# Perceiver layer: context handed over channels first, values' weights loaded beside the queries, exponentials two pieces ahead

## The chip, the core and the metric

One core of a Trainium2 chip runs the whole program. The metric is the device time of one launch in microseconds, the median of the runs. TensorE (PE, with PEld for its weight loads), VectorE (DVE), ScalarE (ACT) and GpSimd (POOL) each work through a queue of their own in program order; SyncE (SP) issues most DMAs. They meet only through semaphores written out by hand.

## What is computed

A layer with a cross-attention, a self-attention and a mixture of experts, each added to `x`. The change touches the first, and the ends of the queries' stage in front of it.

```python
def cross_attention(text_hidden, vision_tokens, vision_mask, Wq, Wk, Wv, Wo):   # (2,256,512), (2,4096,256)
    q = (text_hidden @ Wq).reshape(B, T_text, 16, 128).transpose(0, 2, 1, 3)
    k = (vision_tokens @ Wk).reshape(B, T_vis, 8, 128).transpose(0, 2, 1, 3)    # each used by 2 query heads
    v = (vision_tokens @ Wv).reshape(B, T_vis, 8, 128).transpose(0, 2, 1, 3)
    scores = einsum('bhtd,bhsd->bhts', q, k) / sqrt(128)
    attn = softmax(where(mask, scores, -inf))
    return einsum('bhts,bhsd->bhtd', attn, v) ... @ Wo
x = x + cross_attention(layernorm(x), ctx_1024, mask, ...)
x = x + self_attention(layernorm(x), ...)
x = x + experts(layernorm(x), ...)
```

## The kernel before

The program has four blocks that follow one another: `queries`, `cross`, `selfattn`, `experts`. Every fp32 factor of a product is split into a high part (a copy rounded to fp32r, made by ACT) and a low part (the rest, made by DVE or POOL by a subtraction), and each product is three matmuls: low by high, high by low, high by high.

`queries` layer-norms `x`, makes the queries of all 16 heads, and stores them in DRAM. Beside this SP loads the context of batch 0, raw, into `prob`, 16 pieces of 256 KB (`context_piece`, L144).

`cross` works on one batch after the other. Its pieces:

- `first_part(b)` makes the values. The context arrives with the tokens on the partitions, so PE turns it by transposes against an identity (`context_turn`, L925): 8 blocks of 512 tokens, each with 2 x 4 transposes into two banks of the PSUM ring of 4 (`ring`). ACT copies a bank to `ctxh` (`context_high`, L626), DVE subtracts to `ctxl` and frees the bank (`context_low`, L786). The values' weights are loaded by SP at the start of the block in batch 0 (L404, `values_weight`), ACT makes their high part (`values_weight_high`, L633), DVE the low part (`values_weight_low`, L791). `values_make` (L937) makes 64 products of six matmuls over 512 columns, in two passes (`quad` 0 and 1) over the 32 chunks of 128 tokens; DVE copies each from the ring (`values_out`, L800) and SP stores them in pairs to `v_dram` (L417). DVE waits in `values_out` until the store of the pair two before has landed (`v_st`). The block's turn comes `CTX_LAG` = 2 loop steps after its load and its values `V_LAG` = 4 steps after it.
- `group(...)` makes keys (`keys_make`, L945) and scores (`score`, L956) of head pair u+1, while it turns the exponentials of pair u (`turn`, L965: four transposes per chunk k of 128 tokens, 32 chunks) and multiplies them with the values (`pv`, L975, two chunks later). In a group u = 8b + g - 1. Its chunk k on ACT is the copy `pt_high` (L589), on DVE the subtraction `pt_low` (L741). There are PT = 3 banks for the turned chunks: `turn(k)` waits for `pt_low(k-3)`, and `pv(k)` for `pt_low(k)`.
- The exponentials are in place in `prob` and `more`, [128 rows, 4096 tokens] for each of four tiles t. `exp_piece(u, n, t)` (L575) does one piece of one tile; the pieces are token blocks 0, 1, 2, 3-4, 5-6 and 7 (`PIECES`), and `turn(u, k)` waits at the first chunk of a piece until all four tiles of it are done (k = 0, 4, 8, 12, 20, 28). Piece 0 comes ahead of the group; the others stand in ACT's queue beside the chunks right in front of their use (`BESIDE`, `exp_ahead`), so piece 1 goes with chunks 0 to 3, and turn(4) needs its last quarter.
- Six of the seven groups of a batch that have `pv` run in a loop (g = 2 to 7) and start with two `keys_make` and four `project` (L914, the output product of the pair before). The group of g = 1 (`op` false) has no `project` in front of its first turn.
- Group 8b - 1 for b = 1 has its turns and products inside `first_part(1)`, beside the values of batch 1; there the context's loads go piece by piece into the parts of `prob` that were just turned (SP waits for `pt_full`). The very last group (u = 15) has turns, `pv` and no scores.

`more` is a tensor of `cross` alone; `prob` is shared with the blocks around it.

Of the kernel before, what the change touches and what calls it, by code (L numbers as in the profile page):

```python
# [13 lines left out]
P = 128  # L14
# [95 lines left out]
def queries(nc, x, wq, ctx_in, q_dram, X, ident, prob):  # L110
# [6 lines left out]
    with ExitStack() as ctx:  # L117
# [118 lines left out]
def cross(nc, ctx_in, mask, wk, wv, wo, q_dram, v_dram, attn_w, X, ident, prob):  # L236
# [19 lines left out]
    BESIDE = {1: (0,), 2: (1,), 3: (2,), 5: (3, 4), 7: (5, 6)}  # L256
# [6 lines left out]
    CTX_LAG, V_LAG = 2, 4  # L263

    def ctx_at(n, c):
        return c if n == 0 else (n * 2 + c if n < 2 else 4 + (n - 2) * (CC + NC) + 2 + c)

    def v_at(n, q):
        if n < SB - 2:
            return 4 + n * (CC + NC) + q + (CC if q >= 2 else 0)  # L270
        return 4 + (SB - 2) * (CC + NC) + (n - (SB - 2)) * NC + q

    FIRST = CC * SB + SCH * QUADS
# [27 lines left out]
    with ExitStack() as ctx:  # L301
# [6 lines left out]
        more = t_.sb("more", [P, RT, S])  # L308
# [22 lines left out]
        def wv_raw(quad):  # L331
            return more[:, :, (0, 3)[quad] * BANK:((0, 3)[quad] + 1) * BANK]
# [11 lines left out]
        def wv_part(ring, quad, c):  # L344
# [7 lines left out]
                 "pv_done", "o_hi", "o_lo", "mask_ok", "inv_chain", "any_chain", "scores_seen")  # L352
# [21 lines left out]
        def ctx_count(b, n, c):  # L374
            return b * ((CC + HKV) * SB) + n * CC + c + 1

        def k_count(b, u, n):
            return (b + 1) * (CC * SB) + u * SB + (n + 1)
# [14 lines left out]
        def _(sp):  # L393
# [30 lines left out]
            for b in range(B):  # L424
                u0 = b * HKV

                if b == 0:
                    values_weight(0)
                    values_weight(1)
# [8 lines left out]
                for n in range(SB + V_LAG):  # L438
                    if b and n < SB:
# [6 lines left out]
                        if n == 3:  # L446
                            sp.wait_ge(s["wv_ld"], (b * QUADS + 1) * 16)
                            values_weight(1)
                        if n >= 2:

                            sp.wait_ge(ctx_ld[n % 2], n // 2 * (RT * 16))
                        for r in range(RT):
                            sp.dma_start(*context_piece(prob, ctx_in, b, n, r)).then_inc(ctx_ld[n % 2], 16)
# [3 lines left out]
                    if n >= V_LAG:  # L457
                        for q in range(NC):
                            values_store(b, (n - V_LAG) * NC + q, 0, v_at(n - V_LAG, q))
# [4 lines left out]
                for n in range(SCH):  # L464
                    values_store(b, n, 1, CC * SB + SCH + n)
# [102 lines left out]
        def _(act):  # L568
# [8 lines left out]
            def exp_ahead(u, n, q):  # L577

                for at, blocks in BESIDE.items():
                    if n in blocks:  # L580
                        chunk = blocks.index(n) * NC + q
                        if (chunk + 1) % len(blocks) == 0:
                            exp_piece(u, at, chunk // len(blocks))
# [1470 lines left out]
```

## Time and profile before

| | us |
|---|---|
| median of 3 runs | 2091.35 (2087.42 to 2095.75) |
| profiled execution, device time | 2088.11 |
| its span | 2086.2 |
| PE busy | 1974.1 (95%) |
| DVE busy | 1137.2 (55%) |
| ACT busy | 988.0 (47%) |
| POOL busy | 314.4 (15%) |

In the trace the queries end at 63.5, `cross` runs from 66.7 to 1487, with batch 1 from 727 on, then come self-attention and the experts. PE is the engine that is busy nearly all the time, so what counts is how much work PE has and where it stands still. A row of the timeline gives start, duration, engine, line, what it writes and reads, how many like instructions are merged, and in brackets the idle time of that engine just before, with what ended it. The time between the starts of two rows is what an instruction costs its engine; the duration of one matmul is longer, since they are pipelined.

### The profile page before, as it was taken

The page shows a single profiled execution, that of the slowest core. Times are in us where ns is not written, and L with a number is a line of the kernel's source. Part 1 is how long each engine was busy: PE and PEld are TensorE (multiplying, and loading weights), DVE is VectorE, ACT ScalarE, POOL GpSimd, SP SyncE. Part 2 cuts the span into 40 slices and gives each one's busy share as a digit, 9 for nine tenths or more (in the row PEclk, how much of TensorE's full clock was granted, in tenths as well). Part 3 has the DMA queues.
Part 4 walks back from the last instruction along what each step waited for, and adds up shares of the span by engine and source line. Part 5 has one row for each costly group of instructions (what it writes and reads, how often), then busy time and mean ns, then how long its engine had stood idle before and what let it go on. Part 6 is the DMA issues. An engine that isn't in the chain of part 4 may idle for free. (4 is left out here: it accounts for less than half of the span.)

```text
span 2086.2 us, 32487 instructions
## 1 busy us (share of the span) xinstructions
PE 1974.1 (95%) x10420; PEld 1634.4 (78%) x10420; DVE 1137.2 (55%) x2532; ACT 988.0 (47%) x2092; POOL 314.4 (15%) x252
## 2 busy tenths in 40 slices
PE   7899999999999989999999999998698899999998
PEld 5687877877877778878777877877564588999997
DVE  3457676666666655666676666766757531000002
ACT  3202766665676572055665666676435342122111
POOL 0200111211211113011112211211314210000001
PEclk9899999999999999999999999999899999999999
DMA  7452111111111145501111111102200816466542
GB/s 217 164 188 85 35 45 38 35 48 38 48 31 39 41 134 181 180 24 44 36 43 38 34 48 38 49 25 62 86 0 0 294 57 251 177 243 259 203 177 63
DMA packets 127151, 198.09 MB, mean 95 GB/s; under 512 B 12461, under 2 KB 69989, under 8 KB 122976
## 3 DMA queue, kind: packets, MB, share of 16 engines
q1 hardware_dynamic: 123120, 188.59, 27.3%
q10 hardware_dynamic: 2672, 4.55, 0.7%
q0 software_dynamic: 1280, 3.93, 0.6%
q8 instruction: 46, 0.75, 0.2%
q14 instruction: 33, 0.27, 0.0%
HBM read 151.50 MB, written 45.81 MB: 95 GB/s over the span
## 5 line engine op out<-in xcount | busy, mean ns | idle before, releaser
L741 DVE TENSOR_TENSOR crs_ptl<-crs_tp,crs_pth 128x512 fp32r<-128x512 f32 x512 | 352.7, 689 | 228.2 <-ACT crs_pth L589 227.7
L589 ACT ACTIVATE crs_pth<-crs_tp 128x512 fp32r<-128x512 f32 x504 | 300.6, 597 | 283.7 <-PE crs_tp L965 280.5
L510 POOL TENSOR_TENSOR crs_vl<-crs_vraw,crs_vh 128x512 fp32r<-128x512 f32 x128 | 165.0, 1289 | 1110.5 <-ACT crs_vh L596 1110.5
L965 PE MATMUL crs_tp<-all_ident,crs_prob 128*128 128x128 f32 x1024 | 199.4, 277 | 39.5 <-ACT crs_more L575 39.5
L956 PE MATMUL crs_ring<-crs_kh,crs_ql 128*128 128x512 f32 x512 | 235.3, 460 | 0.0
L965 PEld LDWEIGHTS crs_tp<-all_ident,crs_prob 128*128 128x128 f32 x1024 | 140.9, 141 | 116.3 <-ACT crs_more L575 55.6
L975 PE MATMUL crs_ov<-crs_ptl,crs_vh 128*128 128x512 f32 x512 | 210.5, 411 | 2.0 <-DVE crs_ptl L741 1.5
L975 PE MATMUL crs_ov<-crs_pth,crs_vh 128*128 128x512 f32 x512 | 203.5, 397 | 0.0
L956 PE MATMUL crs_ring<-crs_kh,crs_qh 128*128 128x512 f32 x512 | 202.9, 396 | 0.0
L956 PE MATMUL crs_ring<-crs_kl,crs_qh 128*128 128x512 f32 x512 | 202.1, 395 | 0.0
L975 PE MATMUL crs_ov<-crs_pth,crs_vl 128*128 128x512 f32 x512 | 201.7, 394 | 0.0
L965 PE MATMUL crs_tp<-all_ident,crs_more 128*128 128x128 f32 x1024 | 197.8, 275 | 0.0
L575 ACT ACTIVATE crs_prob<-crs_prob,crs_nmax 128x512 f32<-128x512 f32 (+1 forms) x192 | 165.1, 860 | 65.3 <-DVE crs_nmax L756 65.3
L751 DVE CUSTOM_DVE_ANT_0 crs_prob<-crs_ring,crs_maskb 128x512 f32<-128x512 f32 x256 | 172.5, 682 | 0.5
L751 DVE CUSTOM_DVE_ANT_0 crs_more<-crs_ring,crs_maskb 128x512 f32<-128x512 f32 x256 | 172.5, 682 | 0.0
L1726 DVE TENSOR_SCALAR ex_yT<-moe_bank,moe_b_cols 128x160 f32<-128x160 f32 x32 | 10.8, 379 | 286.9 <-PE moe_bank L1997 286.9
L575 ACT ACTIVATE crs_more<-crs_more,crs_nmax 128x512 f32<-128x512 f32 (+1 forms) x192 | 166.0, 865 | 0.0
L1813 ACT ACTIVATE ex_hT<-moe_bank,moe_b_cols 128x160 f32<-128x160 f32 x128 | 43.5, 390 | 247.4 <-PE moe_bank L1973 247.4
L745 DVE TENSOR_TENSOR crs_kl<-crs_ring,crs_kh 128x512 fp32r<-128x512 f32 x128 | 88.4, 690 | 125.9 <-ACT crs_kh L600 125.9
L1973 PE MATMUL moe_bank<-moe_bufT,moe_w 128*128 128x160 f32 x1024 | 146.9, 304 | 0.6 <-ACT moe_bufT L1808 0.6
L1973 PEld LDWEIGHTS moe_bank<-moe_bufT,moe_w 128*128 128x128 f32 x1024 | 142.1, 193 | 4.0 <-issue 3.0
L965 PEld LDWEIGHTS crs_tp<-all_ident,crs_more 128*128 128x128 f32 x1024 | 129.4, 142 | 0.0
(270 smaller groups left out, 3446.4 us busy)
## 6 DMA issues: line engine op xcount, KB each, us to landing
moe_w<-in_L_ffn_w SPq DMA_DIRECT2D x48, 1024.0 KB, 11.9
v_scratch<-crs_more SPq DMA_DIRECT2D x64, 512.0 KB, 2.9
crs_vraw<-v_scratch SPq DMA_DIRECT2D x128, 256.0 KB, 2.7
ex_w<-in_L_ffn_w SPq DMA_DIRECT2D x16, 1024.0 KB, 13.8
crs_prob<-in_ctx SPq DMA_DIRECT2D x32, 256.0 KB, 4.0
crs_wo<-in_L_xattn_Wo SPq DMA_DIRECT2D x16, 512.0 KB, 4.1
moe_w<-in_L_ffn_sw SPq DMA_DIRECT2D x8, 1024.0 KB, 12.9
qry_wq<-in_L_xattn_Wq SPq DMA_DIRECT2D x16, 256.0 KB, 4.2
```

The source lines that it names most:

```text
L510: nc.gpsimd.tensor_tensor(vl[:, n % VR, :, :], vraw[:, :, :], vh[:, n % VR, :, :].bitcast(F32), ALU.subtract).then_inc(s["v_lo"], 1)
L575: act.activation(w, w, ACT.Exp, bias=nmax[:, t:t + 1], accum_out=rs[:, t, PIECE_OF[n]:PIECE_OF[n] + 1]).then_inc(s["p_ready"], 1)
L589: act.activation(pth[:, k % PT, :], tp[k % PT][:, :], ACT.Copy).then_inc(s["pt_hi"], 1)
L741: v.tensor_tensor(ptl[:, k % PT, :], tp[k % PT][:, :], pth[:, k % PT, :].bitcast(F32), ALU.subtract).then_inc(s["pt_lo"], 1)
L745: v.tensor_tensor(kl[:, n % KR, :], ring[k_at(n, op) % RING][:, :], kh[:, n % KR, :].bitcast(F32), ALU.subtract).then_inc(s["ring_free"], 1)
L751: v.tensor_tensor_reduce(probs(t, n * BANK, (n + 1) * BANK), ring[at % RING][:, :], maskb[:, n * BANK:(n + 1) * BANK], op0=ALU.add, op1=AL ...
L956: m = pe.matmul(ring[at % RING][:, :], a[:, t // RT, rows], w[:, n % KR, :], start=i == 0, stop=i == 2)
L965: m = pe.transpose(tp[k % PT][:, t * P:(t + 1) * P], probs(t, k * P, (k + 1) * P), ident[:, :])
L975: m = pe.matmul(ov[:, :], a[:, k // NC % VR, k % NC, :], w[:, k % PT, :], start=k == 0 and i == 0, stop=k == SCH - 1 and i == 2)
L1726: m = v.tensor_scalar(yT[:, c, :], y_ps[c // 2][:, c % 2 * SL:(c % 2 + 1) * SL], b_cols[:, bass.ds(e * KC + c, 1)], None, ALU.add)
L1813: m = act.activation(hT[:, 2 * n + q, :], h_ps[n % 2][:, q * SL:(q + 1) * SL], ACT.Gelu, bias=b1_cols[:, bass.ds(e * FC + (2 * n + q), 1)])
L1973: m = pe.matmul(h_ps[n % 2][:, q * SL:(q + 1) * SL], w1[i][:, c, fc * P:(fc + 1) * P], bufT[:, i, c, :], start=c == 0, stop=c == KC - 1)
```

## The change

- The host hands the context over as [batch, channel, token] instead of [batch, token, channel]. `context_piece` then loads one block of 512 tokens with the channels on the partitions, one DMA of 512 KB with rows of 2 KB, where two DMAs of 256 KB with rows of 1 KB stood. `context_turn` is gone, and with it the ring's places for it. `context_high` and `context_low` now read the raw block from `prob`, both halves of the channels in one instruction of 128x1024; a semaphore `ctx_lo` of its own tells PE. In batch 1 the wait for the load stands in front of `context_high` on ACT; before it stood in front of the transposes on PE.
- `more` is allocated ahead of `queries`, and the two loads of the values' weights of batch 0 (512 KB each) stand in the SP queue of `queries` behind the context's.
- The lags are `CTX_LAG` = 0 and 1, `V_LAG` = 1 and 3 for batch 0 and 1.
- The exponentials are placed earlier: of piece 1, two quarters stand ahead of chunk 0, the others beside chunks 0 and 1; piece 2 beside chunks 2 to 5, piece 3-4 beside 6 to 9, piece 5-6 beside 11, 13, 15, 17, piece 7 beside 19, 21, 23, 25. In the group of g = 1, all of piece 0 comes ahead of the first key copy.

```diff
-def context_piece(prob, ctx_in, b, n, r):
-
-    k = BANK // P // RT
-    return (prob[:, r, bass.ds(n * BANK, BANK)].rearrange("p (k c) -> p k c", c=DC),
-            ctx_in[bass.ds(b, 1), bass.ds(n * BANK + r * (k * P), k * P), :].rearrange("o (k p) c -> p (o k) c", p=P))
+def context_piece(prob, ctx_in, b, n):
+
+    cols = slice(n * BANK, (n + 1) * BANK) if isinstance(n, int) else bass.ds(n * BANK, BANK)
+    return prob[:, :, cols], ctx_in[b, :, cols].rearrange("(c p) n -> p c n", p=P)
...
                 for i in range(SB * SLOTS // H):
-                    for half in range(RT):
-                        sp.dma_start(*context_piece(prob, ctx_in, 0, r * (SB * SLOTS // H) + i, half)).then_inc(ctx_ld, 16)
-            sp.wait_ge(ctx_ld, SB * RT * 16)
+                    sp.dma_start(*context_piece(prob, ctx_in, 0, r * (SB * SLOTS // H) + i)).then_inc(ctx_ld, 16)
+            for i in range(2):
+                sp.dma_start(values_weight_place(more, i), wv[:, i * BANK:(i + 1) * BANK].rearrange("(c p) n -> p c n", p=P)).then_inc(ctx_ld, 16)
+            sp.wait_ge(ctx_ld, (SB + 2) * 16)
...
-    BESIDE = {1: (0,), 2: (1,), 3: (2,), 5: (3, 4), 7: (5, 6)}
+    BESIDE = {0: (1, 2), 1: (1, 3)}
+    BESIDE.update({2 + t: (2, t) for t in range(GRP * RT)})
+    BESIDE.update({6 + t: (3, t) for t in range(GRP * RT)})
+    BESIDE.update({11 + 2 * t: (5, t) for t in range(GRP * RT)})
+    BESIDE.update({19 + 2 * t: (7, t) for t in range(GRP * RT)})
...
-    CTX_LAG, V_LAG = 2, 4
...
+    CTX_LAG, V_LAG = (0, 1), (1, 3)
...
+    FIRST = SCH * QUADS
...
-            def context_high(b, n, c):
-                at = first_op(b) + ctx_at(n, c)
-                act.wait_ge(s["ring_full"], first_base(b) + at + 1)
-                act.activation(ctxh[:, c, n * BANK:(n + 1) * BANK], ring[at % RING][:, :], ACT.Copy).then_inc(s["keys_hi"], 1)
+            def context_high(b, n):
+                if b:
+                    act.wait_ge(ctx_ld[n % 2], (n // 2 + 1) * 16)
+
+                    act.wait_ge(s["ring_full"], first_base(b))
+                cols = slice(n * BANK, (n + 1) * BANK)
+                act.activation(ctxh[:, :, cols], prob[:, :, cols], ACT.Copy).then_inc(s["keys_hi"], 1)
...
                         for t in range(QT):
                             exp_piece(u, 0, t)
+                        exp_piece(u, 1, 0)
+                        exp_piece(u, 1, 1)
...
                     exp_piece(u, 0, 3)
+                    exp_piece(u, 1, 0)
+                    exp_piece(u, 1, 1)
                 else:
+                    for t in range(QT):
+                        exp_piece(u, 0, t)
                     for n in range(AHEAD):
-                        exp_piece(u, 0, n)
                         keys_high(R, n, op)
-                    exp_piece(u, 0, 2)
-                    exp_piece(u, 0, 3)
+                        exp_piece(u, 1, n)
...
-            def context_low(b, n, c):
-                at = first_op(b) + ctx_at(n, c)
-                v.wait_ge(s["keys_hi"], ctx_count(b, n, c))
-                v.tensor_tensor(ctxl[:, c, n * BANK:(n + 1) * BANK], ring[at % RING][:, :],
-                                ctxh[:, c, n * BANK:(n + 1) * BANK].bitcast(F32), ALU.subtract).then_inc(s["ring_free"], 1)
+            def context_low(b, n):
+                cols = slice(n * BANK, (n + 1) * BANK)
+                v.wait_ge(s["keys_hi"], ctx_count(b, n))
+                v.tensor_tensor(ctxl[:, :, cols], prob[:, :, cols], ctxh[:, :, cols].bitcast(F32), ALU.subtract).then_inc(s["ctx_lo"], 1)
...
-            def context_turn(b, n, c):
-                at = first_op(b) + ctx_at(n, c)
-                if b and c == 0:
-                    pe.wait_ge(ctx_ld[n % 2], (n // 2 + 1) * (RT * 16))
-                if first_base(b) + at >= RING:
-                    free(first_base(b), at)
-                for q in range(NC):
-                    col = n * BANK + q % 2 * DC + c * P
-                    m = pe.transpose(ring[at % RING][:, q * P:(q + 1) * P], prob[:, q // 2, col:col + P], ident[:, :])
-                m.then_inc(s["ring_full"], 1)
...
                 if quad == 0 and k % NC == 0:
 
-                    pe.wait_ge(s["ring_free"], first_base(b) + first_op(b) + ctx_at(k // NC, CC - 1) + 1)
-                free(first_base(b), at)
+                    pe.wait_ge(s["ctx_lo"], b * SB + k // NC + 1)
+                if first_base(b) + at >= RING:
+                    free(first_base(b), at)
```

## Rows read from the trace of the kernel before

**Rows 1.** The page, busy us by engine (share of span) and instructions.
```profile
PE 1974.1 (95%) x10420; PEld 1634.4 (78%) x10420; DVE 1137.2 (55%) x2532; ACT 988.0 (47%) x2092; POOL 314.4 (15%) x252
```
**Rows 2.** Waits of the whole span: waited for, us in total, times, longest.
```profile
PE crs_tp L965 <- ACT crs_more L575: 39.5, 23, 3.6
```
**Rows 3.** Timeline where the block with batch 0 starts, all engines.
```profile
66.72 0.90 SPq L404 DMA_DIRECT2D crs_more<-in_L_xattn_Wv  x2
...
71.85 1.06 ACT L633 ACTIVATE crs_kh<-crs_more 128x1024 fp32r<-128x1024 f32 x1 [7.70 <-DMA crs_more<-in_L_xattn_Wv]
...
72.93 1.23 DVE L791 TENSOR_TENSOR crs_kl<-crs_more,crs_kh 128x1024 fp32r<-128x1024 f32 x1 [13.09 <-ACT crs_kh L633]
...
74.08 1.28 DVE L786 TENSOR_TENSOR crs_ctxl<-crs_ring,crs_ctxh 128x512 fp32r<-128x512 f32 x2
...
75.28 1.49 DVE L791 TENSOR_TENSOR crs_kl<-crs_more,crs_kh 128x1024 fp32r<-128x1024 f32 x1
...
75.46 1.19 PE L937 MATMUL crs_ring<-crs_kh,crs_ctxl 128*128 128x512 f32 x2 [5.05 <-DVE crs_ctxl L786]
```
**Rows 4.** Timeline of PE in batch 0: two blocks' transposes, products of values between.
```profile
80.11 1.03 PE L925 MATMUL crs_ring<-all_ident,crs_prob 128*128 128x128 f32 x8
80.91 0.70 PE L937 MATMUL crs_ring<-crs_kh,crs_ctxl 128*128 128x512 f32 x2
...
86.48 1.03 PE L925 MATMUL crs_ring<-all_ident,crs_prob 128*128 128x128 f32 x8
```
**Rows 5.** Windows: length, busy us by engine, granted PEclk, DMA share, GB/s.
```profile
75.40:79.00 3.60, 3.54 (x8) 2.81 (x9) 3.17 (x4) 0.39 (x1) 3.52 (x2) 0.50 0.18 66
...
750.00:755.00 5.00, 2.75 (x10) 2.35 (x11) 1.79 (x3) 3.31 (x7) 1.28 (x1) 0.68 0.08 26
```
**Rows 6.** Timeline at the start of a group of the loop, batch 0.
```profile
283.34 0.60 ACT L589 ACTIVATE crs_pth<-crs_tp 128x512 fp32r<-128x512 f32 x1 [1.67 <-PE crs_tp L965]
...
283.84 0.71 ACT L575 ACTIVATE crs_prob<-crs_prob,crs_nmax 128x512 f32<-128x512 f32 x1
...
284.54 0.58 ACT L589 ACTIVATE crs_pth<-crs_tp 128x512 fp32r<-128x512 f32 x1
...
287.59 0.68 DVE L741 TENSOR_TENSOR crs_ptl<-crs_tp,crs_pth 128x512 fp32r<-128x512 f32 x1
...
288.38 0.73 ACT L575 ACTIVATE crs_more<-crs_more,crs_nmax 128x512 f32<-128x512 f32 x1
...
289.26 0.44 PE L965 MATMUL crs_tp<-all_ident,crs_prob 128*128 128x128 f32 x2 [1.86 <-ACT crs_more L575]
```
**Rows 7.** Waits of PE in 430 to 700 us: four groups of the loop.
```profile
PE crs_tp L965 <- ACT crs_more L575: 7.5, 4, 1.9
```
**Rows 8.** Timeline of PE, group of g = 1, batch 0 and then batch 1.
```profile
207.78 0.44 PE L965 MATMUL crs_tp<-all_ident,crs_prob 128*128 128x128 f32 x2 [2.37 <-ACT crs_more L575]
...
214.80 0.44 PE L965 MATMUL crs_tp<-all_ident,crs_prob 128*128 128x128 f32 x2 [0.69 <-ACT crs_more L575]
...
919.26 0.44 PE L965 MATMUL crs_tp<-all_ident,crs_prob 128*128 128x128 f32 x2 [1.87 <-ACT crs_more L575]
```
**Rows 9.** Timeline of ACT and of PE in the first part of batch 1.
```profile
731.90 0.60 ACT L589 ACTIVATE crs_pth<-crs_tp 128x512 fp32r<-128x512 f32 x1 [1.46 <-PE crs_tp L965]
...
736.81 0.44 PE L965 MATMUL crs_tp<-all_ident,crs_prob 128*128 128x128 f32 x2 [1.39 <-ACT crs_more L575]
...
752.25 0.69 PE L965 MATMUL crs_tp<-all_ident,crs_prob 128*128 128x128 f32 x2 [3.64 <-ACT crs_more L575]
```
**Rows 10.** DMA issues in 722 to 830 us: KB each, median us to landing.
```profile
crs_prob<-in_ctx SPq DMA_DIRECT2D x16, 256.0 KB, 3.1
...
crs_more<-in_L_xattn_Wv SPq DMA_DIRECT2D x2, 512.0 KB, 3.7
```
**Rows 11.** Timeline of PE and of ACT in the last group.
```profile
1454.98 0.69 PE L965 MATMUL crs_tp<-all_ident,crs_prob 128*128 128x128 f32 x2 [2.17 <-ACT crs_more L575]
...
1476.48 0.63 ACT L596 ACTIVATE crs_vh<-crs_vraw 128x512 fp32r<-128x512 f32 x1 [1.35 <-DMA crs_vraw<-v_scratch]
```

More of the change, by code:

```diff
@@ L107, in raw_weight_load, with queries @@
                       w[r * k * P:(r + 1) * k * P, :].rearrange("(c p) n -> p c n", p=P)).then_inc(sem, 16)
-def queries(nc, x, wq, ctx_in, q_dram, X, ident, prob):
+def queries(nc, x, wq, ctx_in, wv, q_dram, X, ident, prob, more):
     SLOTS = 4
@@ L233, in _, with cross @@
                     m.then_inc(q_ps, 1)
-def cross(nc, ctx_in, mask, wk, wv, wo, q_dram, v_dram, attn_w, X, ident, prob):
+def cross(nc, ctx_in, mask, wk, wv, wo, q_dram, v_dram, attn_w, X, ident, prob, more):
     RING = 4
@@ L331, in wv_raw @@
         def wv_raw(quad):
-            return more[:, :, (0, 3)[quad] * BANK:((0, 3)[quad] + 1) * BANK]
+            return values_weight_place(more, quad)
         def v_pair(n):
@@ L437, in _ @@
                     output_weight(HKV - 1)
-                for n in range(SB + V_LAG):
+                for n in range(SB + V_LAG[b]):
                     if b and n < SB:
@@ L577, in exp_ahead @@
             def exp_ahead(u, n, q):
[L579 to L583, printed above, removed]
+                if n * NC + q in BESIDE:
+                    exp_piece(u, *BESIDE[n * NC + q])
             def pt_high(u, k):
@@ L636, in first_part @@
                 u = b * HKV - 1
-                for n in range(SB + V_LAG):
+                for n in range(SB + V_LAG[b]):
                     if b and n == 0:
@@ L653, in first_part @@
                                 values_high(u, n + 1)
-                        if q == 1 and CTX_LAG <= n < SB + CTX_LAG:
-                            for c in range(CC):
-                                context_high(b, n - CTX_LAG, c)
+                        if q == 1 and CTX_LAG[b] <= n < SB + CTX_LAG[b]:
+                            context_high(b, n - CTX_LAG[b])
                 if b:
@@ L816, in first_part @@
                 R = first_base(b)
-                for n in range(SB + V_LAG):
+                for n in range(SB + V_LAG[b]):
                     if b and n == 0:
@@ L828, in first_part @@
                             pt_low(u, n * NC + q)
-                        if n >= V_LAG:
-                            values_out(b, (n - V_LAG) * NC + q, v_at(n - V_LAG, q))
-                        if q == 1 and CTX_LAG <= n < SB + CTX_LAG:
-                            for c in range(CC):
-                                context_low(b, n - CTX_LAG, c)
+                        if n >= V_LAG[b]:
+                            k = (n - V_LAG[b]) * NC + q
+                            values_out(b, k, k)
+                        if q == 1 and CTX_LAG[b] <= n < SB + CTX_LAG[b]:
+                            context_low(b, n - CTX_LAG[b])
                 if b:
@@ L837, in first_part @@
                 for i in range(SCH):
[L838 removed]
+                    values_out(b, SCH + i, SCH + i)
                     if i >= SCH // 2 and i % 2 == 0:
@@ L982, in first_part @@
                         project(first_base(b), t, t, u - 1)
-                for n in range(SB + V_LAG):
+                for n in range(SB + V_LAG[b]):
                     for q in range(NC):
@@ L987, in first_part @@
                             turn(u, k)
[L988 to L989 removed]
+                        if n >= V_LAG[b]:
+                            i = k - V_LAG[b] * NC
+                            values_make(b, i, 0, i)
                         if b and LAG <= k < SCH + LAG:
                             pv(u, k - LAG)
[L992 to L994 removed]
                 for k in range(SCH):
[L996 removed]
+                    values_make(b, k, 1, SCH + k)
             def group(b, u, R, op, pv_too):
@@ L2028, in perceiver @@
             prob = Tensors(nc, three, "crs").sb("prob", [P, RT, S])
-            queries(nc, a["x"], a["L0_xattn_Wq"], a["ctx_1024"], q_dram, X, ident, prob)
+            two = three.enter_context(ExitStack())
+            more = Tensors(nc, two, "crs").sb("more", [P, RT, S])
+            queries(nc, a["x"], a["L0_xattn_Wq"], a["ctx_1024"], a["L0_xattn_Wv"], q_dram, X, ident, prob, more)
             cross(nc, a["ctx_1024"], a["mask_BxS2_bf1"], a["L0_xattn_Wk"], a["L0_xattn_Wv"], a["L0_xattn_Wo"], q_dram, v_dram,
-                  [a[f"L0_attn_{n}_w"] for n in ("q", "k", "v")], X, ident, prob)
+                  [a[f"L0_attn_{n}_w"] for n in ("q", "k", "v")], X, ident, prob, more)
+            two.close()
             selfattn(nc, a, X, ident, prob)
```

48 lines of the change are left out of this document (18 added, 30 removed).

## The prediction

> **What bounds the kernel now.** First the page: PE is busy 1974.1 us of the span, DVE 55%, ACT 47% [rows 1]. Then the waits of PE over the span: in `cross` nearly all of its idle time is one thing, `turn` standing for the last quarter of a piece of exponentials, 39.5 us in 23 waits [rows 2]. Third the timeline around each kind of these waits, with ACT's rows beside PE's: ACT isn't the bound of a group, it has the exponentials queued too near their use. So the change can gain in three coins: work that leaves PE (the transposes), idle time of PE (exponentials, the start of batch 0), and the slow clock that follows a long idle time. Self-attention and experts are untouched.
>
> **Start of batch 0: 5.0 us.** Here nothing moves until the weights have landed: SP issues them at 66.72, ACT starts at 71.85, and PE's first product waits until 75.46 [rows 3]. With both loads landed inside the queries, ACT begins at 66.7: weights 1.06, context block 1.06 by 68.8. DVE does the weights' low part from 67.9 (1.23), then the block's low part (1.23 to 1.49, the same operation on the same shape, [rows 3]): 70.3 to 70.6. PE starts at 70.4 instead of 75.46. The two loads, and that the context's 16 DMAs become 8, cost nothing in the queries: they stand last in SP's queue, with no load of the queries behind them, and have some 10 us before the block ends; if that cover failed, the end of the block would wait for them, at most the 3.7 us that such a load takes [rows 10], behind a gain of 5.0.
>
> **Transposes of batch 0: 4.8 us.** Eight transposes take PE 80.11 to 80.91, 0.80 [rows 4]. The first two blocks' lie in the stretch above, six follow: 6 x 0.80. What is late next is `ctx_lo`: between two blocks' transposes four products take 86.48 - 80.91 = 5.57. DVE now has the block's low part behind two `values_out`: two products 2.8, latency and copy 0.8, low part 1.2 to 1.5, so it is ready 4.8 to 5.1 after the block before has begun. It just fits.
>
> **Loop groups: 22.4 us.** In each, turn(4) stands 1.86 [rows 6], four groups in 430 to 700 have 7.5 together [rows 7], and there are 12. The exponential that it waits for starts at 288.38, with a start-to-start cost of 0.70 for an exponential and 0.50 for a copy [rows 6]. Two of the four now go ahead of chunk 0, where ACT stands idle 1.67 before 283.34 [rows 6]; they need 1.40, so the first copy isn't late. The other two then end near 286.0, 3 us earlier, and PE, whose wait began at 289.26 - 1.86 = 287.4, goes on. What is late next: pv(2) needs the subtraction of chunk 2, which starts at 287.59 and ends at 288.3 [rows 6]; PE will ask for it at 287.4 + 0.44 (turn) + 0.69 (score: three matmuls of 5.57 / 24 = 0.23, [rows 4]) = 288.5. A margin of 0.2, with no exponential in front of that copy that wasn't there before. Later chunks take PE 1.8 each (0.44 + 0.69 + 0.69) and ACT about 1.2 with its exponential (1.6 with a double one), so ACT gets ahead. Bounds: 0 (all of the wait passes to DVE) and 1.86; I take 1.86 since each date comes from this very stretch.
>
> **Groups of g = 1: 3.5 us.** turn(0) stands 2.37, turn(4) 0.69 in batch 0 and 1.87 in batch 1 [rows 8]. With two key copies (0.5 each) moved behind the last quarter of piece 0, turn(0) comes 1.0 earlier. The first chunk copy then waits for two copies and two exponentials, 2.4 us; worked through by the same steps, PE reaches turn(5) 2.0 earlier in batch 0 and 1.5 in batch 1, held by DVE's subtractions. Bounds 2 and 6.
>
> **First part of batch 1: 7.6 us.** Until chunk 12 there are no products of values, and ACT is the bound: it works without a pause from 731.90 on, and turn(12) stands 3.64 until 752.25 [rows 9]. Two exponentials go into the 1.46 of idle time before 731.90. Step by step with ACT's new order (context blocks 0 and 1 included, at 1.0 each, as 2 x 0.5 before), turn(12) goes at 749.8: 2.4. After it seven blocks' transposes are gone, 7 x 0.80 = 5.6. In 750 to 755 the clock was 0.68 on average [rows 5], from the stand of 3.64; without it 1.3. Against it: `context_low` of block 1 now stands before chunk 10's subtraction, 1.0; and PE gets a new stand of 2.9 before pv(8), since two copies of weights (1.0 each) stand in front of chunk 8's copy. The stand of 3.64 restarts at the slow clock (a pair of transposes 0.69 instead of 0.44, [rows 9]), that of 1.86 doesn't (0.44, [rows 6]); 2.9 lies between, so I take half of 1.3. 2.4 + 5.6 + 1.3 - 1.0 - 0.7 = 7.6. Bounds 2 and 12. The wait for the load, moved to ACT, has the next chunks' copies behind it. Piece and weights are issued at about 735; a piece takes 3.1, 512 KB 3.7 [rows 10], and ACT asks at 739.5. From the fourth block on ACT asks some 5 us after the issue. I take 0, the price of lateness is below.
>
> **Last group: 3.0 us.** ACT is the bound up to turn(12), which stands 2.17 and restarts slowly (0.69 for what takes 0.44) [rows 11]. Two exponentials ahead and the slow clock saved would be near 4; but at the end ACT already waits for the values' load (1.35 at 1476.48, [rows 11]), a chain that doesn't get shorter. Bounds 1 and 4.5.
>
> **A page weighed.** `context_low` took PSUM in two instructions, 74.08 to 75.28, 1.20 start to start; the same subtraction from SBUF took 1.23 once and 1.49 when POOL was at work on the mask [rows 3]. The Trainium skill, page "Perfetto Trace Analysis", section "Optimizing Scalar/DVE Operations", says that DVE's overhead is about 60 ns on SBUF against 125 on PSUM, so one instruction from SBUF should be cheaper than two from PSUM. By it the block would take about 0.2 less and the sum gain nothing, since PE is the bound. The same section says that GpSimd and DVE share an SBUF read port, which speaks against the change.
>
> **Sum.** 5.0 + 4.8 + 22.4 + 3.5 + 7.6 + 3.0 = 46.3. The profiled execution took 2088.1 (span 2086.2), so 2041.8; the median of the runs is 3.2 above it, so 2045.
>
> **The rivals.**
> - *The stand moves to DVE.* In the loop groups the margin at pv(2) is 0.2 and DVE's subtractions follow one another; if half of each 1.86 comes back there: 2045 + 11 = 2056. For it: in the first part pv already stands on DVE between turns. Against it: the dates above.
> - *The first part of batch 1 gains nothing.* The new stand at pv(8) drops the clock, and the stores of the values, now one block earlier in SP's queue beside the second load of weights, hold DVE: 2053.
> - *DVE and POOL get in each other's way.* The page's rule on the shared port, as a mechanism of this kernel: the mask's conversion on POOL now starts beside the context blocks of batch 0. If a low part took 2.2 instead of 1.49 [rows 3], each of seven blocks would be 0.3 to 0.7 late on PE: 2045 + 5 = 2050.
> - *Slower: ACT waits for the context.* In batch 1 each of eight blocks' loads has ACT's queue behind it. ACT asks about 5 us after the issue; up to 5 it costs nothing, beyond it each microsecond costs up to 8. At 7 us it is 2061; the point from which the kernel is slower is 11 us, and at 12 us it is 2101. Against it: 3.1 and 3.7 in this very stretch, at half the DMA's capacity [rows 10].
> - *It doesn't do what it says.* ACT has no idle time where the exponentials go, and chunk 0's copy comes late by as much as turn(4) is early. Only the transposes and the start are left: 2091.35 - 5.0 - 4.8 - 5.6 = 2076. Against it: 1.67 and 1.46 of idle time at that place [rows 6, 9].
>
> **How the numbers follow.** Forecast 0.58, stand on DVE 0.16, first part without gain 0.10, port 0.07, ACT waits for the context 0.06 (0.02 of it beyond 11 us), no effect 0.03. The likeliest's own range, from the terms' bounds, is 2037 to 2052. With the DVE case the range is 2035 to 2058; outside are the last two cases and the tails. About 0.5% (10.4 us) is what a measurement of this kernel can tell from no change: faster by more 0.95, within 0.03, slower 0.02.
>
> **What would show it.** PE's first product of values near 70.4; no rows of transposes in the first part; no wait of PE for L575 in the loop groups and their period 1.9 shorter; a PE that asks for pv(2) without a wait for DVE; in the first part of batch 1, turn(12) about 2.4 us closer to the group's first turn; ACT's waits for DMA of the context at zero. The prediction is wrong if PE's idle time shows up under DVE L741 instead, if the products of values in batch 0 wait for `ctx_lo`, or if the queries' stage itself becomes longer.

## The result and the profile after

| | before | after |
|---|---|---|
| median of the runs, us | 2090.20 (2087.42 to 2095.75, 4 runs) | 2028.38 (2026.92 to 2031.33, 4 runs) |
| profiled execution: device time, span, us | 2088.1, 2086.2 | 2026.92, 2025.2 |
| PE busy, us | 1974.1 [rows 1] | 1945.5 |

The ratio is 0.9704, 95% interval 0.9686 to 0.9721: faster by 61.8 us. The forecast was 2045 with a range of 2035 to 2058. The direction was right; the time lies 6.6 us below the range.

First the page, with the same line as [rows 1]: 128 matmul instructions are gone, the transposes of 16 context blocks, and PE's busy time fell by 28.6 us. As the span fell by 61, somewhat more than half of the gain is idle time of PE.

```profile
PE 1945.5 (96%) x10292; PEld 1611.8 (80%) x10292; DVE 1131.0 (56%) x2516; ACT 983.2 (49%) x2076; POOL 316.4 (16%) x252
```

Then the waits of PE (waited for, us in total, times, longest). The wait of [rows 2], 39.5 us in 23, is down to the second line. The first has grown, from 1.5 in 4: `pv` standing for DVE's subtractions. Both lines are of the whole span.

```profile
PE crs_ov L970 <- DVE crs_ptl L747: 8.8, 11, 2.5
...
PE crs_tp L960 <- ACT crs_more L576: 3.0, 2, 1.6
```

The start of batch 0, where [rows 3] showed the block waiting for the weights. ACT begins 0.02 us after SP's first issue, without a wait for a DMA, and PE's first product of values comes at 71.54.

```profile
67.93 0.82 SPq L432 DMA_DIRECT2D crs_more<-in_mask_BxS_bf  x2
67.95 1.06 ACT L634 ACTIVATE crs_kh<-crs_more 128x1024 fp32r<-128x1024 f32 x1 [2.60 <-PEq L122]
...
70.18 1.22 DVE L792 TENSOR_TENSOR crs_ctxl<-crs_prob,crs_ctxh 128x1024 fp32r<-128x1024 f32 x1
...
71.54 1.19 PE L932 MATMUL crs_ring<-crs_kh,crs_ctxl 128*128 128x512 f32 x2 [6.82 <-DVE crs_ctxl L792]
```

The loop groups next, in windows (length, busy us by engine, granted PEclk, DMA share, GB/s). First two neighbouring groups before, from one group's maxima to the next's, and inside the second of them a stretch at half clock:

```profile
425.86:500.26 74.40, 72.53 (x382) 59.76 (x381) 51.20 (x115) 49.07 (x100) 13.36 (x10) 1.00 0.14 41
500.26:576.24 75.98, 74.11 (x382) 60.98 (x381) 51.31 (x114) 49.05 (x100) 13.35 (x10) 0.98 0.14 40
...
512.90:516.30 3.40, 3.40 (x13) 2.71 (x11) 1.39 (x3) 1.32 (x4) 1.28 (x1) 0.50 0.20 52
```

and the same two groups after:

```profile
409.85:482.05 72.20, 72.20 (x382) 59.82 (x381) 51.01 (x114) 48.85 (x100) 13.38 (x10) 1.00 0.14 42
482.05:554.25 72.20, 72.20 (x382) 59.82 (x381) 51.01 (x115) 48.85 (x100) 13.38 (x10) 1.00 0.14 42
```

```profile
512.46 0.44 PE L965 MATMUL crs_tp<-all_ident,crs_prob 128*128 128x128 f32 x2 [1.87 <-ACT crs_more L575]
```

After, all 12 take 72.2, PE is busy in the whole of each, and the clock is 1.00.

From the starts of the same instructions in both traces, stage by stage (us; E1 and E2 are the two halves of the change alone, below):

| stage | forecast | after | E1, exponentials | E2, context |
|---|---|---|---|---|
| queries, to their last matmul | 0 | +1.2 | +1.5 | +0.4 |
| to the first product of values | -5.0 | -5.1 | -0.1 | -5.1 |
| rest of the values, batch 0 | -4.8 | -5.5 | +0.8 | -5.3 |
| two groups of g = 1 | -3.5 | -3.9 | -3.9 | -0.1 |
| 12 loop groups | -22.4 | **-34.5** | -34.7 | +1.8 |
| first part, batch 1 | -7.6 | -9.1 | -2.0 | -4.4 |
| last group | -3.0 | -2.9 | -2.0 | +0.3 |
| self-attention | 0 | -1.5 | -0.3 | +0.2 |
| experts | 0 | +0.2 | -1.9 | +0.5 |
| span | -46.3 | -61.1 | -42.5 | -11.8 |

Each row of the table ends where the next begins: batch 0's values at the maxima of the first group's scores, a group at the next group's maxima, the last group where self-attention begins. Of the 14.8 us of the span that are missing in the forecast 12.1 lie in one line, the loop groups. The median was missed by another 1.8 us: the forecast put it 3.2 above the profiled execution, as in the kernel before, and it is 1.5 above.

### The profile page after: what moved, and what is told of

It reads as the page before. It is cut to its first block and busy times, and to the rows that moved or that the text cites. A ratio compares the mean times of both kernels' runs of the same rounds, so it can differ in the third digit from the quotient of the medians.

```text
span 2025.2 us, 32167 instructions
## 1 busy us (share of the span) xinstructions
PE 1945.5 (96%) x10292; PEld 1611.8 (80%) x10292; DVE 1131.0 (56%) x2516; ACT 983.2 (49%) x2076; POOL 316.4 (16%) x252
## 5 line engine op out<-in xcount | busy, mean ns | idle before, releaser
L960 PE MATMUL crs_tp<-all_ident,crs_prob 128*128 128x128 f32 x1024 | 195.1, 272 | 3.0 <-ACT crs_more L576 3.0
L1719 DVE TENSOR_SCALAR ex_yT<-moe_bank,moe_b_cols 128x160 f32<-128x160 f32 x32 | 10.9, 379 | 285.7 <-PE moe_bank L1990 285.6
```

Source lines behind the costliest of these rows:

```text
L960: m = pe.transpose(tp[k % PT][:, t * P:(t + 1) * P], probs(t, k * P, (k + 1) * P), ident[:, :])
```

## The experiments

The lags, the copies and the loads that are named in the expectations are those of the change. Every kernel of this section was timed five times, E3 seven; a gain in us is of the medians, against the kernel before on the same chip.

**E1 and E2: the halves alone.** E1 is the kernel before with the new order of the exponentials:

```diff
-    BESIDE = {1: (0,), 2: (1,), 3: (2,), 5: (3, 4), 7: (5, 6)}
+    BESIDE = {0: (1, 2), 1: (1, 3)}
+    BESIDE.update({2 + t: (2, t) for t in range(GRP * RT)})
...
                         for t in range(QT):
                             exp_piece(u, 0, t)
+                        exp_piece(u, 1, 0)
+                        exp_piece(u, 1, 1)
...
```

> The kernel before with the new order of the exponentials alone; the context is still turned on the chip and the values' weights still load inside cross. Theory of the prediction (each loop group gains the idle time shown, 1.86 us, and no clock): 12 x 1.86 + 3.5 + 3.0 + about 3 of the first part of batch 1 = 32 us, so 2058. Theory of the clock (the stand costs 2.20 us by issue, and in 5 of 12 groups it also costs about 1.6 us of half clock behind it): 34.5 + 3.9 + 2.9 + 3 = 44 us, so 2046, with every loop group at the period of 72.2 us. If the two halves of the change need each other, the loop groups here keep part of their 74.4 or 76.0 us.

E2 is the changed kernel with these lines as they were before.

> The changed kernel with the old order of the exponentials: context by channels and weights beside the queries alone. Both theories: the first product of values near 71.5 us (3.9 earlier), batch 0 another 5.5 earlier, the first part of batch 1 about 5.6 to 7 earlier, loop groups as before at 74.4 or 76.0 us; in all 15 to 17 us, so 2074. With the first kernel of this call it should add up to the 61.8 us of the whole change; a sum below 57 would mean that the halves need each other.

E1 took 2045.99 (2043.32 to 2049.91), ratio 0.9793 [0.9779, 0.9808], a gain of 44.1 us: the number of the clock theory, and 12 below that of the prediction's. (The 2.20 us that the expectation gives one stand are two stands, as shown below.) E2 took 2075.81 (2074.28 to 2079.01), ratio 0.9934 [0.9920, 0.9947], a gain of 14.2. Together they gain 58.3, so neither half needs the other for its gain. Six loop groups each, before, in E1, in E2 and after:

```profile
277.00:726.60 449.60, 438.41 (x2282) 360.99 (x2281) 307.42 (x684) 294.14 (x599) 79.43 (x59) 0.99 0.14 39
```
```profile
278.00:710.00 432.00, 432.00 (x2277) 358.06 (x2276) 305.54 (x682) 292.15 (x599) 79.58 (x59) 1.00 0.14 41
```
```profile
266.50:717.80 451.30, 440.08 (x2282) 362.10 (x2280) 307.49 (x684) 294.33 (x599) 79.46 (x59) 0.99 0.14 39
```
```profile
265.40:698.60 433.20, 433.20 (x2282) 358.91 (x2280) 306.04 (x684) 292.82 (x599) 79.56 (x59) 1.00 0.14 41
```

(E1's window is 1.1 us short of the six groups, which take 433.1.) So the loop term belongs to the exponentials' order alone. E2 shows a thing more: its loop groups have the same stand as before, six of the 12 take 76.0 instead of five, and they are not the same ones. Whether one stand costs clock is therefore not fixed by the code of the group.

**E3: the stand stays, PE is kept at work in it.** The kernel before with six matmuls in the stand, their result thrown away:

```diff
             def turn(u, k, fill=False):
-                if k % NC == 0 and k // NC in PIECES:
-                    pe.wait_ge(s["p_ready"], ...)
                 if k >= PT:
                     pe.wait_ge(s["pt_lo"], u * SCH + (k - PT + 1))
+                if fill and k == NC:
+                    for i in range(6):
+                        pe.matmul(tp[k % PT][:, :], ctxh[:, 0, 0:P], ctxh[:, 0, 0:BANK], start=True, stop=True)
+                if k % NC == 0 and k // NC in PIECES:
+                    pe.wait_ge(s["p_ready"], ...)
```

> The kernel before, with six matmuls of 512 columns (results thrown away, overwritten by the transposes behind them) in every group, between turn(4)'s wait for its buffer and its wait for the exponentials: the stand is as long as before, but PE works in it for 6 x 0.23 = 1.4 us of its 2.0. Theory of the clock: the five loop groups of 76.0 us fall to 74.2, a gain of 8 us, so 2082, or a little more if also the slower restart of every group goes. Theory of the prediction (the clock has no part in a stand of 1.86): nothing, 2090; 2092 or above if the six matmuls reach past the stand.

2084.01 (2081.35 to 2084.31), ratio 0.9970 [0.9959, 0.9981]: 6.0 us faster, although PE does 14 times 1.4 us of useless work and turn(4) in the loop groups starts when it did. The timeline of PE at one turn(4) (idle time before it in brackets), and six groups in one window:

```profile
286.56 1.53 PE L964 MATMUL crs_tp<-crs_ctxh 128*128 128x512 f32 x6
288.59 0.44 PE L968 MATMUL crs_tp<-all_ident,crs_prob 128*128 128x128 f32 x2 [0.49 <-ACT crs_more L575]
...
276.31:722.84 446.53, 443.60 (x2318) 365.27 (x2317) 307.22 (x684) 294.15 (x599) 79.50 (x59) 1.00 0.14 40
```

446.53 / 6 = 74.42, the period of an undisturbed group before, and all 12 have it: 7.9 us less than before in the loops, where 8 was expected. The rest was given back where the fillers do harm or chance decides. The groups of g = 1 took 0.5 and 1.0 more. In batch 0 the stand before turn(4) is 0.69, shorter than the fillers [rows 8]. In batch 1 a stretch at half clock began behind turn(0), at 911.1, where the kernel before had none, and turn(4) came right behind the fillers. The first part of batch 1 took 1.9 more, and its half clock lasted 6.8 us instead of 3.4. That the clock is worth 8 us in the loops is shown: the time of turn(4) is unchanged here, only PE's work before it differs.

**E4: the stand made shorter.** The kernel before with the exponentials one ahead:

```diff
-    BESIDE = {1: (0,), 2: (1,), 3: (2,), 5: (3, 4), 7: (5, 6)}
+    BESIDE = {t - 1: (1, t) for t in range(1, GRP * RT)}
+    BESIDE.update({3 + t: (2, t) for t in range(GRP * RT)})
...
+                        exp_piece(u, 1, 0)
...
```

> The kernel before with the exponentials one ahead instead of two (the last of piece 1 stands before chunk 3's copy instead of behind it): the stand before turn(4) is shorter by about 1.2 us, not gone. Theory of the prediction: 12 x 1.2 + 4 for the groups outside the loops = 18 us, so 2072, and the time of a group follows the stand in proportion. Theory of the clock: a stand of 0.8 us costs no clock in any group, so 8 us more, 2064; periods of the loop groups all near 73.0 us.

2056.63 (2055.32 to 2058.10), ratio 0.9841 [0.9828, 0.9855], a gain of 33.4, more than either theory said.

```profile
287.96 0.44 PE L969 MATMUL crs_tp<-all_ident,crs_prob 128*128 128x128 f32 x2 [0.68 <-ACT crs_more L579]
...
422.96:495.97 73.01, 72.33 (x382) 59.81 (x381) 51.12 (x114) 48.95 (x100) 13.38 (x10) 1.00 0.15 41
```

The idle time before turn(4) fell from 1.86 to 0.68 and the period from 74.4 to 73.0: 1.39 us for 1.18 of idle time shown. The other 0.21 is a second stand, before turn(28), of which more below; it is gone here. No loop group lost clock. In the loops this is 24.6 us, 12 times these 1.39 and the 8.0 of the clock, near what the clock theory had (22); the surplus lies outside, 9 us where I had put 4: the groups of g = 1 gained 2.0 and 1.6, the first part 2.3, the last group 3.1. One exponential ahead brings all that the first and last parts have to give, the second only helps in the loops.

**E5: the weights' loads back in the block.**

```diff
-            for i in range(2):
-                sp.dma_start(values_weight_place(more, i), wv[:, i * BANK:(i + 1) * BANK].rearrange("(c p) n -> p c n", p=P)).then_inc(ctx_ld, 16)
...
+                    values_weight(0)
+                    values_weight(1)
                     for r in range(2):
                         sp.dma_start(mask_u8[r], ...)
...
```

> The changed kernel with the loads of the values' weights back in cross. If the start's gain is the landing of these loads, as the prediction has it, ACT's copy starts 5.1 us after cross begins instead of at once, the first product of values moves from 71.5 to about 76.7 us and the kernel takes 2033.5. If the queries of the changed kernel were 1.2 us longer because of these loads beside them, they end at 63.1 here, and the time is 2032.3. If the start's gain were the context copied without a transpose and not the loads, the first product stays below 73 us and the time at 2029 to 2030.

2034.69 (2032.26 to 2035.21), ratio 0.9737 [0.9723, 0.9750], 6.3 above the change's median.

```profile
70.19 1.06 ACT L634 ACTIVATE crs_kh<-crs_more 128x1024 fp32r<-128x1024 f32 x1 [7.66 <-DMA crs_more<-in_L_xattn_Wv]
...
73.79 1.19 PE L932 MATMUL crs_ring<-crs_kh,crs_ctxl 128*128 128x512 f32 x2 [11.89 <-DVE crs_ctxl L792]
```

From the queries' last matmul to the first product of values are 12.28 us, in the changed kernel 7.21: the loads are worth 5.07, and the third theory (no loss without them) falls. The queries ended at 61.5 here, but that isn't the loads either: over all kernels run they end between 61.5 and 64.7, and at 64.7 in E1, whose queries are those of the kernel before. The 1.2 us of the table are this spread.

**E7: the lags.** The halves gain 58.3 by their medians, the whole 61.8. In the traces most of the difference is in the first part of batch 1 (2.0 + 4.4 against 9.1).

```diff
-    CTX_LAG, V_LAG = (0, 1), (1, 3)
+    CTX_LAG, V_LAG = (0, 2), (1, 4)
```

> The changed kernel with the lags of the kernel before in batch 1 (context copied two blocks behind its load instead of one, values made from the fifth block on instead of the fourth). The two halves of the change gained 44.1 and 14.2 us alone and 61.7 together, and the 2.7 us of the 3.4 that are more than the sum lie in the first part of batch 1 (2.0 and 4.4 us alone, 9.1 together). If it is the lags, which put four more products of values beside the exponentials where ACT is the bound, and which do nothing while PE stands on turn(12) anyway, the first part is about 2.7 us longer here: 2031.1. If the lags have no part in it: 2028.4.

2030.26 (2026.27 to 2030.66), ratio 0.9709 [0.9696, 0.9723]. The first part took 172.53, against 172.80, so the lags are not it; the 1.9 us by the medians can't be told from nothing, and in the profiles self-attention, which no kernel touches, differs by 2.7. What the traces show instead, first in E2:

```profile
744.40 0.69 PE L953 MATMUL crs_tp<-all_ident,crs_prob 128*128 128x128 f32 x2 [3.61 <-ACT crs_more L572]
...
743.40:750.20 6.80, 5.80 (x18) 4.83 (x19) 1.93 (x3) 2.07 (x4) 1.28 (x1) 0.50 0.14 39
```

With the transposes gone and the exponentials where they were, turn(12) goes 1.0 us later after the part's start than before (26.6 against 25.6), its stand is as long as in [rows 9], and the half clock lasts 6.8 us instead of 3.4, 1.7 us more. But E1 has no half clock in this part at all, where the kernel before has 3.4 us: in the sum of the halves the clock cancels, and it doesn't explain the 2.7. Behind turn(12) E1 has 2.6 us of idle time of PE, 1.2 for DVE's copies of values and 1.4 for one of its subtractions; the kernel before has 0.4 there, and the changed kernel, as E2, none:

```profile
732.50:890.10 157.60, 155.00 (x749) 128.70 (x748) 103.57 (x195) 37.90 (x73) 26.08 (x13) 1.00 0.47 153
```
```profile
722.90:871.40 148.50, 148.50 (x693) 123.06 (x692) 100.23 (x185) 36.23 (x63) 26.07 (x13) 1.00 0.51 162
```

These 2.2 us that E1 pays and the whole change doesn't, and the 1.0 of E2, are of the size of the 2.7 in question. I take them as the likely cause; no run separates it.

**E6, E8, E9: better than both?** In the first part after, `pv` of chunk 8 stands 2.47, and a stretch at half clock follows:

```profile
719.80 0.50 PE L970 MATMUL crs_ov<-crs_ptl,crs_vh 128*128 128x512 f32 x1 [2.47 <-DVE crs_ptl L747]
...
720.40:723.80 3.40, 3.40 (x14) 2.80 (x13) 1.75 (x2) 3.40 (x7) 0.00 (x0) 0.50 0.17 40
```

> The changed kernel with two copies of ACT moved in the first part of batch 1: the values' weights (high and low part) from before chunk 8 to behind chunk 10, the output weights' copy from before chunk 8 to before chunk 16. In the changed kernel pv(7) stands 1.5 us and pv(8) 2.5 us behind them, and a half-clock stretch follows. If the copies in front of chunk 8 are the cause, both copies' 2.0 us leave the stand, no half-clock stretch follows, and the first part is 2.5 to 3.6 us shorter: 2025 to 2026. If ACT is simply full there, the stand moves to a later chunk and the time stays at 2028.4; if the first product of values then waits for its weights, it is 1 to 2 us longer.

> The changed kernel with 24 transposes of the identity (results thrown away) at the start of cross, where PE stands until 71.5 us. The changed kernel runs at half clock from 68.4 to 75.2 us, 3.7 us of it under products of values, which costs half of that. Theory: PE busy until 71.5 keeps or regains the clock: 1.8 us less, 2026.6. Rival: the clock is lost by the idle time before cross already (64.7 to 68) and the transposes run at half clock, 0.17 to 0.23 us each, 4.1 to 5.5 us, past 71.5: the same or up to 2 us more, 2028.4 to 2030.4.

> The changed kernel with the 24 transposes at the start of cross, and in the first part of batch 1 only the output weights' copy moved from before chunk 8 to before chunk 16 (the values' weights stay where the changed kernel has them, since with them moved the first product of values stood 2.9 us for its weights). If each of the two copies before chunk 8 has its own 1.0 us in the stand of 2.5 before pv(8), that stand falls to 1.5, and the first part is 1.0 us shorter, 2.6 if the half-clock stretch at 720 goes too; with 1.0 us at the start the kernel takes 2025 to 2026. Rival: the first product of values, which comes 1.0 us earlier, waits for DVE's low part instead, and the first part keeps its 172.8 us: 2027.5.

The edits, E6 and E9 on ACT's queue and E8 on PE's (E6 moves `values_weight_low` on DVE in the same way; E9 has of the first block the move of `output_weight_high` alone, with E8's fill):

```diff
-                    if n == (2 if b else 0):
+                    if not b and n == 0:
                         values_weight_high(b, 0)
-                    if b and n == 2:
+                    if b and n == 4:
                         output_weight_high(u, first_base(b) + QT)
...
+                        if b and n == 2 and q == 2:
+                            values_weight_high(b, 0)
```
```diff
+                if b == 0:
+                    for i in range(24):
+                        pe.transpose(tp[0][:, i % 4 * P:(i % 4 + 1) * P], ident[:, :], ident[:, :])
```

| | median, us | ratio to before | first part of batch 1, us |
|---|---|---|---|
| change | 2028.38 | 0.9704 [0.9686, 0.9721] | 172.8 |
| E6 | 2028.74 (2028.21 to 2035.15) | 0.9720 [0.9705, 0.9736] | 174.3 |
| E8 | 2027.83 (2024.97 to 2031.25) | 0.9709 [0.9695, 0.9722] | 173.0 |
| E9 | 2026.68 (2026.43 to 2029.17) | 0.9704 [0.9691, 0.9717] | 171.2 |

None is better by more than can be measured. E6: the stand at chunk 8 went, and a longer one came where the products begin (first line). E9: with the output weights' copy gone from before chunk 8 the stand there is still 2.40 (second line), so that copy was never in it. DVE's rows in the changed kernel tell why: the subtraction of chunk 8 stands behind DVE's low part of the values' weights, which starts when ACT's high part is done; ACT copies the output weights in its shadow.

```profile
722.15 1.22 PE L936 MATMUL crs_ring<-crs_kh,crs_ctxl 128*128 128x512 f32 x2 [2.95 <-DVE crs_kl L798]
```
```profile
717.44 0.50 PE L970 MATMUL crs_ov<-crs_ptl,crs_vh 128*128 128x512 f32 x1 [2.40 <-DVE crs_ptl L747]
```
```profile
716.72 1.27 POOL L511 TENSOR_TENSOR crs_vl<-crs_vraw,crs_vh 128x512 fp32r<-128x512 f32 x1 [6.09 <-ACT crs_vh L594]
...
717.49 1.04 ACT L615 ACTIVATE crs_woh<-crs_wo 128x1024 fp32r<-128x1024 f32 x1
...
717.62 1.46 DVE L796 TENSOR_TENSOR crs_kl<-crs_more,crs_kh 128x1024 fp32r<-128x1024 f32 x1 [1.90 <-ACT crs_kh L634]
719.05 0.69 DVE L747 TENSOR_TENSOR crs_ptl<-crs_tp,crs_pth 128x512 fp32r<-128x512 f32 x1
```

The 1.6 us that E9's first part is shorter are the half-clock stretch, which didn't come behind its stand of 2.40; the span of its profiled execution is only 0.4 shorter, since self-attention and experts took 2.8 us more. In E8 the clock came back while the transposes ran (granted 0.50 from 66.8 to 70.2, 1.00 from 70.8), where the changed kernel has 0.50 until 75.2:

```profile
66.61 4.48 PE L977 MATMUL crs_tp<-all_ident 128*128 128x128 f32 x24 [3.26 <-PEq L122]
70.84 0.71 PE L932 MATMUL crs_ring<-crs_kh,crs_ctxl 128*128 128x512 f32 x2
...
66.80:70.20 3.40, 3.40 (x18) 3.40 (x17) 2.36 (x2) 3.40 (x4) 0.00 (x0) 0.50 0.66 170
70.80:74.20 3.40, 3.40 (x18) 2.82 (x17) 1.01 (x2) 3.40 (x5) 2.58 (x1) 1.00 0.66 233
```

The products began 7.88 us behind the queries' last matmul, 0.67 later than in the changed kernel, and from there to the first group's maxima 128.77 us went by, 1.05 less: both theories had a part of it. But E9 has the same 24 transposes, and there they ran at half clock throughout, 5.0 us start to start:

```profile
65.66 5.35 PE L977 MATMUL crs_tp<-all_ident 128*128 128x128 f32 x24 [3.25 <-PEq L122]
70.66 1.03 PE L932 MATMUL crs_ring<-crs_kh,crs_ctxl 128*128 128x512 f32 x2
```

The products began 8.64 behind the queries' last matmul, and the same stretch took 130.15, 0.3 more than in the changed kernel (129.82) and between two kernels in which nothing was edited there (E6 129.64, E7 130.85). So the 1.0 of E8 is not shown to be the fill's.

## Why the prediction was wrong, point by point

**The step that failed: the loop groups' term, 12 x 1.86 = 22.4.** It measured 34.5. That the exponentials' place ends the stand, that nothing takes its place and that all 12 gain was right; what a group loses to late exponentials was read wrongly, in three ways.

*The clock, 8.0 us.* The prediction says that the stand of 3.64 restarts at the slow clock and "that of 1.86 doesn't", from one restart [rows 6]. Five of the 12 stands of this length were followed by a stretch at 0.50, 1.6 us each (76.0 against 74.4). Two of them stand in the very stretch of [rows 7], from 512.9 and 663.1 us on; that group of rows counts waits and can't show them, the periods of the groups do. E3 is the proof: turn(4) as late as before, the clock kept, 7.9 us.

*A second stand, 2.5 us.* turn(28), the first of the last piece, also waits for its exponentials, in all 12 loop groups. The matmul rows of PE show no idle time there, since the one before is modelled to end 0.40 behind its start. The starts show it: 0.39 between the last `pv` and turn(28), where PE running through takes 0.23. The row of the weight load (PEld) names the wait:

```profile
488.15 0.72 ACT L575 ACTIVATE crs_more<-crs_more,crs_nmax 128x512 f32<-128x512 f32 x1
...
488.62 0.40 PE L975 MATMUL crs_ov<-crs_pth,crs_vh 128*128 128x512 f32 x1
...
489.00 0.20 PEld L965 LDWEIGHTS crs_tp<-all_ident,crs_prob 128*128 128x128 f32 x2 [0.43 <-ACT crs_more L575]
489.01 0.44 PE L965 MATMUL crs_tp<-all_ident,crs_prob 128*128 128x128 f32 x2
```

and after:

```profile
470.62 0.39 PE L970 MATMUL crs_ov<-crs_pth,crs_vh 128*128 128x512 f32 x1
470.86 0.38 PE L960 MATMUL crs_tp<-all_ident,crs_prob 128*128 128x128 f32 x2
```

With the slower first pair (0.44 for 0.38) it is 0.21 a group: it stands in the kernel before, E2 and E3, and is gone after, in E1 and in E4.

*The idle time shown, 1.6 us.* 12 x 0.13. From turn(0) to turn(8) a group that lost no clock took 15.28 before and 13.29 after: the stand whose idle time reads 1.86 is worth 1.99. In E4 one of 0.68 is worth 0.82. The idle time is counted from the modelled end of the matmul before, 0.40 behind its start, but the next could have started 0.23 behind it. The prediction's "Bounds: 0 (all of the wait passes to DVE) and 1.86" took the idle time of one row for the most that a group can gain.

**The start of batch 0, 5.0.** Right: 5.1, and E5 gives 5.07 for the loads alone. The first product came at 71.54 and not near 70.4 because the queries ended 1.2 later.

**Transposes of batch 0, 4.8.** 5.5 by the change and 5.3 by E2. The mechanism was right: PE is busy without a gap behind the first products and never waits for `ctx_lo`. A block's transposes are worth 0.9 rather than 0.80.

**Groups of g = 1, 3.5.** 3.9 (2.1 and 1.7 for 2.0 and 1.5); E1 gives the same. turn(0) still stands 1.4 and 1.6 us for its exponentials, the two waits of 3.0 together in the lines above.

**First part of batch 1, 7.6.** 9.1. The new stand before pv(8) came (2.47 for 2.9), and so did the half clock behind it, that I had counted by half. But its cause was named wrongly: of the "two copies of weights" only one is in it, and DVE's 1.46 with it (E9); and pv(7) stands 1.52 ahead of it, which no step had. The sign "turn(12) about 2.4 us closer to the group's first turn" failed: it is 1.3 closer (19.65 for 20.99), since the half clock from 720.4 on now lies mostly ahead of turn(12), and before it lay behind. Behind turn(12) 7.7 us were won: seven blocks' transposes at 0.87 by starts, 6.1, about 1.0 by that shift of the half clock, and 0.4 of waiting for DVE's copies that is gone. ACT waited for the context twice, 0.19 at 711.84 and 3.76 at the eighth block (776.13); PE has no wait for `ctx_lo` behind either, so this cost nothing, though the prediction's sign was no such wait.

**Last group, 3.0.** 2.9; 2.0 in E1 and 3.1 in E4, so chance has a part of a microsecond in it.

**Outside, 0.** The queries were 1.2 longer and self-attention 1.5 shorter, both within what these stages do from kernel to kernel (queries as above, self-attention 134.7 to 137.4 from first to last matmul).

**The rivals.** The stand did not move to DVE in the loops: PE waits there for nothing. ACT's wait for the context, no effect, and a first part without gain are out as well. The port costs no time here, but the effect on DVE is there. In the eleven traces, DVE's subtraction of 128x1024 from SBUF (the context's and the values' weights' low parts) took 1.21 to 1.23 us in all 91 cases with POOL idle. Of 65 with POOL at work beside it 33 took the same and 32 took longer, 1.30 to 2.01. One of each, in the changed kernel and in E9, both beside POOL's conversion of the mask (in E9 from 70.77 to 85.57):

```profile
73.44 11.88 POOL L525 TENSOR_SCALAR crs_maskb<-crs_more 128x1024 bf16<-128x1024 uint8 x3 [71.89 <-DMA crs_more<-in_mask_BxS_bf]
...
76.91 1.22 DVE L792 TENSOR_TENSOR crs_ctxl<-crs_prob,crs_ctxh 128x1024 fp32r<-128x1024 f32 x1
```
```profile
74.62 2.01 DVE L792 TENSOR_TENSOR crs_ctxl<-crs_prob,crs_ctxh 128x1024 fp32r<-128x1024 f32 x1
```

The 1.46 at chunk 8 is one of them: POOL's subtraction from 716.72 runs beside its first 0.37 us. With the 32 longer ones the traces agree with what the Trainium skill, page "Perfetto Trace Analysis", section "Optimizing Scalar/DVE Operations", says of a read port that GpSimd and DVE share. PE's products of values in batch 0 waited for `ctx_lo` in none of the kernels with the new context, not even behind the 2.01 in E9, so the rival's 5 us did not come. Nor is there the 0.2 us that one instruction from SBUF should save on two from PSUM: by starts the two cost 1.20 (74.08 to 75.28, [rows 3]) and the one 1.15 (72.93 to 74.08); the prediction set a time between starts beside durations.

What no rival allowed for is a gain above the likeliest's: the range's low end held the loop groups, half of the forecast's gain, at 22.4.

## What to carry to other kernels

Size a repeated stand by the period of its loop, not by the idle time before one instruction: list the periods of all repeats beside the granted clock; where they come in two kinds, the difference is a price that only some repeats pay, and it goes with the stand. Look for stands that no matmul row shows, by the starts and in the rows of the weight loads. Where one exponential (or copy) ahead is enough to shorten a stand to 0.7 us, most of the gain is had (33 of 44 us here). Before moving a copy out of a stand, follow what the engine that releases it did before, since a copy in another engine's shadow is free already (E9).

## What the runs showed of the hardware that was not expected

- Behind stands of about 1.9 us PE's clock fell to 0.50 in 5 of 12 repeats in one kernel and in 6 of 12, others, in E2; behind 0.68 and 0.49 in none of 12 each.
- A stand of 2.47 was followed by half clock, one of 2.40 at the same place of another kernel was not.
- Useless transposes at the start of a block ran at half clock (24 in 4.2 us start to start in E8, 5.0 in E9). Counted from the queries' last matmul, the full clock was back after 7.2 us in E8 and 9.3 in E9, without them after 10.9 in the changed kernel; from the queries' end to the first group's maxima that was worth 1.0 us once and nothing once.
- DVE's subtraction of 128x1024 from SBUF took 1.21 to 1.23 us with POOL idle, and up to 2.01 beside POOL, in 32 of 65 cases.
- A stand of 0.16 us at turn(28), in 12 of 12 loop groups, has no idle time in the matmul rows; a stand of 1.86 us by these rows was worth 1.99 of the group's time.
